# Attention and mixture-of-experts layer: gathers in bursts of eight, the last addition by banks, the last store on another queue

## The chip, the cores and the metric

The kernel runs on one core of one Trainium2 chip. Its time is the device time of one execution in microseconds (us); less is better. TensorE (PE in the profile) multiplies matrices into PSUM banks, VectorE (DVE) and ScalarE (ACT) work element by element, GpSimd (POOL) here makes the lists for indirect transfers, and SyncE (SP) issues the plain transfers. Each engine runs its own instructions in order; semaphores tie them together.

## The reference, cut to what matters

Inputs are x (2, 1024, 256), a context (2, 64, 256) and weights, all float32. First comes a cross-attention with 8 heads of 64, whose queries are x and whose keys and values are x and the context; its normalised output is added to x. The second part is the one that the change touches:

```python
x = x + _L0_xattn_ref(ctx_1024, _layernorm(x), mask, ...)
x = x + _L0_ffn_ref(_layernorm(x), ...)

# _L0_ffn_ref(x, ...)
shared_out = (silu(x @ shared_w1) * (x @ shared_w2)) @ shared_w3      # hidden width 1024
scores = sigmoid(x @ router_w)
_, top_idx = top_k(scores + expert_bias, 2)                           # 2 of 16 experts
gates = sum(one_hot(top_idx) * top_scores)
for each expert e:                                                    # hidden width 256
    routed_out += (silu(x @ w1[e]) * (x @ w2[e])) @ w3[e] * gates[:, e]
return shared_out + routed_out
```

The result for every token is its attention result, plus the shared branch, plus the gated results of its two experts.

## The kernel before, in words

The 2048 tokens are 16 tiles of 128 (`NT = 16`). Attention fills the span up to about 490 us and stays untouched. Behind it, the routed branch works on slots: the rows of the tokens are scattered in HBM so that the rows of one expert lie together (GpSimd, L714), 47 slots of 128 rows run through their expert's weights (about 635 to 777 us), and each slot's result is stored in the HBM tensor `slot_results`.

The shared branch has 32 steps n: four groups of 4 tiles (g = n // 8), and in each group 8 parts of the hidden width. A step is `hidden` (8 matmuls, L1062, about 3.4 us), then silu on ScalarE (L1317), then the product on VectorE (L1578), then `down` (8 matmuls, L1077, about 1.7 us), which adds to banks 4 and 5. `down(n)` is run behind `hidden(n + 1)`; behind the last `hidden`, n = 31, `down(30)` and `down(31)` run back to back. Steps 0 to 21 run before the slots. **Steps 22 to 31 run behind them (`BREAK = 22`), and they are the last stretch of the kernel: everything in the change lies there.**

Beside these ten steps the results come back. For each tile n GpSimd issues two gathers (`TOP = 2`, L724), 128 rows each, into one of three buffers (`NGAT = 3`), having waited until the tile three before was combined. VectorE's `combine(n)` (two instructions, L1761) waits for both gathers to land, multiplies by the gates and adds to `x2`. VectorE's order is written out: a product, then combines, up to tile 2j - 2 behind the product of step 22 + j. So tiles 13 and 14 are combined between the products of steps 30 and 31, and tile 15 behind the product of step 31. Last comes `add_shared(3)` (L1584), which waits for the last `down` and adds bank 4 (tiles 12 and 13), then bank 5 (tiles 14 and 15), with one signal behind both. SyncE waits for each tile's combine and stores the tile (L591); before tile 12 it waits for the last addition, so tiles 12 to 15 are stored at the very end.

The scatter loop (L714) waits behind every four tiles (`BURST = 4`), that is eight transfers, until all have landed. The gather loop has no such wait.

Of the kernel before, what the change touches and what calls it, by code (L numbers as in the profile page):

```python
# [29 lines left out]
B, S, D = 2, 1024, 256  # L30
# [3 lines left out]
P = 128  # L34
# [3 lines left out]
NT = B * TQ  # L38
# [8 lines left out]
SU = SH // P  # L47
# [4 lines left out]
NG = NT * P // GR  # L52
TOP = 2
NS = (TOP * NT * P + E * (P - 1)) // P
NGAT = 3
# [13 lines left out]
def wait(eng, sem, value):  # L69

    if isinstance(value, int) and value <= 0:
        return
    eng.wait_ge(sem, value)


def build(nc, x, ctx, mask, ln_x_w, ln_x_b, ln_l_w, ln_l_b, wq, wkv, q_scale, k_scale, wo,
          ln_o_w, ln_o_b, router_w, expert_bias, sw1, sw2, sw3, rw1, rw2, rw3, out, dbg=None):
    es = ExitStack()

    def sb(name, shape, dt=F32, stack=es):  # L80
        return stack.enter_context(nc.sbuf_tensor(name, shape, dt))

    def sem(name):
        return es.enter_context(nc.semaphore(name))
# [80 lines left out]
    x2 = sb("x2", [P, NT, D], stack=ffn)  # L165
# [5 lines left out]
    if nc.sbuf_bytes_remaining > att_end:  # L171
# [78 lines left out]
    hid_made, sil_ready, hid_ready, ysh_made, ysh_added = (sem("hid_made"), sem("sil_ready"), sem("hid_ready"),  # L250
                                                         sem("ysh_made"), sem("ysh_added"))
# [7 lines left out]
    gathered = [sem(f"gathered{i}") for i in range(NGAT)]  # L259
    combined, out_stored = sem("combined"), sem("out_stored")  # L260
# [148 lines left out]
    GB = NG - 1  # L409
# [8 lines left out]
    BURST = 4  # L418
# [40 lines left out]
    def _(sp):  # L459
# [125 lines left out]
        for n in range(NT):  # L585
            sp.wait_ge(combined, n + 1)
            if n == 4 * (GB - 1):
                sp.wait_ge(ysh_added, GB)
            if n == 4 * GB:
                sp.wait_ge(ysh_added, NG)  # L590
            sp.dma_start(out[n % B, (n // B) * P:(n // B + 1) * P, :], x2[:, n, :]).then_inc(out_stored, 16)  # L591
        sp.wait_ge(out_stored, 16 * NT)

# [2 lines left out]
    def _(pool):  # L596
        g = nc.gpsimd
# [68 lines left out]
        for m in range(NCH):  # L666
# [4 lines left out]
            n = TK * m  # L671
# [48 lines left out]
        for n in range(NT):  # L720

            wait(pool, combined, n - NGAT + 1)
            for k in range(TOP):
                g.indirect_dma_start(out=gat[n % NGAT][:, k, :], out_offset=None, in_=ys_dram,  # L724
                                     in_offset=bass.IndirectOffsetOnAxis(ap=posi[:, n, k:k + 1], axis=0)
                                     ).then_inc(gathered[n % NGAT], 16)
# [3 lines left out]
    def _(pe):  # L730
# [275 lines left out]
        def turn_xf(t):  # L1006
            pe.wait_ge(xf_ready, t + 1)
            if t == EARLY:
                pe.wait_ge(o_ready, NCH)
            if t > EARLY:  # L1010
                pe.wait_ge(xf_moved, t)
            for c in range(B):
                for k in range(DK):
                    last = nc.tensor.transpose(turn_bank(t)[:, (c * DK + k) * P:(c * DK + k + 1) * P],
                                               xf[:, 2 * t + c, k * P:(k + 1) * P], ident[:, :])
            last.then_inc(xf_turned, 1)
# [49 lines left out]
        def down(g, u, beside_pair=None):  # L1066
            pe.wait_ge(hid_ready, SU * g + u + 1)
            if g == 0 and u == 0:
                pe.wait_ge(o_ready, NCH)
            if g == 0 and u in (0, 2):  # L1070
                pe.wait_ge(w3s_loaded, 16 if u == 0 else 32)
            if u == 0:
                wait(pe, ysh_added, g)
            for j in range(4):
                if j == 2 and beside_pair is not None:
                    turn_xf(beside_pair)
                last = mm_(bank[4 + j // 2][:, (j % 2) * D:(j % 2 + 1) * D], hbuf[:, u % 4, j * P:(j + 1) * P],  # L1077
                           w3s[:, u, :], start=(u == 0 and j % 2 == 0), stop=(u == SU - 1), skip_group_check=True)
            if u == SU - 1:
                last.then_inc(ysh_made, 1)  # L1080

        def shared(n):

            g, u = divmod(n, SU)
            if u == 0:
                pe.wait_ge(xf_moved, 2 * g + 2)
            now, last = beside(n), beside(n - 2)
            if last == TQ - 1:
                route()
                turn_logits()  # L1090
            if now is not None and now <= EARLY:
                now = None
            if n == 1:
                pe.wait_ge(y_used, EARLY + 1)
            if n == COUNT_AT:
                count_tokens()
            hidden(g, u)
            if now is not None:
                project_o(now)
            for m in down_after(n):  # L1100
                down(*divmod(m, SU), beside(m) if m < n else None)
# [52 lines left out]
    def _(act):  # L1154
# [156 lines left out]
        def shared(n):  # L1311
            last = beside(n - 2)
            if last == TQ - 1:
                copy_logits()
                make_scores()
            act.wait_ge(hid_made, n + 1)
            a(hbuf[:, n % 4, :], hidden_bank(n, 0)[:, :], ACT.Silu).then_inc(sil_ready, 1)  # L1317
            if beside(n - 1) is not None:
                copy_xfT(beside(n - 1))
# [30 lines left out]
        for n in range(BREAK, SU * NG):  # L1350
            shared(n)


    @block.vector
    def _(dve):
# [224 lines left out]
        def add_shared(g):  # L1580
            dve.wait_ge(ysh_made, g + 1)
            for j in range(2):
                rows = x2[:, 4 * g + 2 * j:4 * g + 2 * j + 2, :]
                last = v.tensor_tensor(rows, bank[4 + j][:, :].rearrange("p (c d) -> p c d", c=2), rows, ALU.add)  # L1584
            last.then_inc(ysh_added, 1)
            v.drain()
# [30 lines left out]
        def shared_product():  # L1617

            nonlocal hid
            product(hid // SU, hid % SU)  # L1620
            if hid % SU == 0 and hid:
                add_shared(hid // SU - 1)
            hid += 1
# [150 lines left out]
        while done < NT:  # L1774
            combine(done)
            done += 1
        v.drain()
        add_shared(GB)

    es.close()  # L1780
# [26 lines left out]
```

## Time and profile before

| what | value |
|---|---|
| median of 3 runs | 833.82 us (833.03 to 834.02) |
| the profiled execution, its own time | 838.75 us |
| its span, first to last instruction | 837.0 us |
| TensorE busy | 806.2 us, 96% |
| VectorE, ScalarE, GpSimd busy | 58%, 41%, 39% |
| mean granted clock of TensorE | 0.996 of full |
| last stretch (ten shared steps, 16 tiles gathered and combined) | about 775.6 to 837.0 us |

The profiled execution is 4.93 us longer than the median of the ordinary runs. "Busy" leaves waits out; the view by chain follows the instruction that ended last back through what released it.

### The profile page before, as it was taken

Reading aid. Unit: us, or ns where it says so; the run is one execution under the profiler, and the core shown is the slowest. Engines: PE = TensorE matmul, PEld = TensorE weight load, DVE = VectorE, ACT = ScalarE, POOL = GpSimd, SP = SyncE. Lnnn points to the kernel's source line nnn. Section 1 sums busy time; section 2 is a strip of 40 time slices with the busy share of each in tenths; the row PEclk is TensorE's granted clock in tenths of the full one; section 3 lists DMA queues with packets and bytes.
Section 4 is the critical chain, followed back from the end, with each engine's and each line's share of the span. In section 5 each row is a group of like instructions: output and inputs, shape, how many; then the busy total and the mean of one; then the engine's idle time right before and its main releaser. Section 6 shows DMA issues by size and latency. Waiting matters only on the chain.

```text
span 837.0 us, 12969 instructions
## 1 busy us (share of the span) xinstructions
PE 806.2 (96%) x4354; PEld 492.8 (59%) x4355; DVE 485.8 (58%) x905; ACT 341.4 (41%) x652; POOL 327.0 (39%) x252
## 2 busy tenths in 40 slices
PE   8999988999999999999999999999999999999987
PEld 5444344545545554555454456666557999999544
DVE  4877777776676767777663376647212333433334
ACT  3545364465656555655655321131112333333110
POOL 3000034466665656465666743310661000000463
PEclk9999999999999999999999999999999999999998
DMA  3105600000000000000002002491521232322343
GB/s 114 36 29 182 227 1 1 14 14 14 14 9 7 14 14 14 15 15 14 14 17 74 13 25 63 145 325 64 183 89 64 94 94 89 93 90 79 89 131 95
DMA packets 54117, 55.99 MB, mean 67 GB/s; under 512 B 10666, under 2 KB 49204, under 8 KB 54068
## 3 DMA queue, kind: packets, MB, share of 16 engines
q1 hardware_dynamic: 50980, 46.96, 17.9%
q0 software_dynamic: 3072, 8.39, 3.1%
q8 instruction: 29, 0.48, 0.2%
q14 instruction: 20, 0.16, 0.1%
q10 hardware_dynamic: 16, 0.00, 0.0%
HBM read 36.60 MB, written 18.67 MB: 66 GB/s over the span
## 4 chain that ended last, share of the span: by engine, by line
PE 89%; ACT 4%; DVE 2%; POOL 1%; issue 1%; DVEq 1%; DMA 0%; ACTq 0%; POOLq 0%
PE bank L914 14%; PE bank L1062 13%; PE bank L888 11%; PE bank L762 11%; PE bank L1125 10%; PE bank L1077 7%; PE bank L842 5%; PE bank L1134 5%; PE bank L897 4%; ACT prob L1238 3%; PE bank L968 2%; PE bank L826 2%; PE bank L923 2%; PE bank L1115 1%; POOL acc L680 1%
## 5 line engine op out<-in xcount | busy, mean ns | idle before, releaser
L1238 ACT ACTIVATE prob<-bank,zero 128x512 f32<-128x512 f32 x256 | 158.7, 691 | 103.8 <-PE bank L897 103.2
L1446 DVE TENSOR_REDUCE mx<-bank 128x1 f32<-128x512 f32 x256 | 164.4, 686 | 54.2 <-PE bank L842 53.9
L680 POOL TENSOR_TENSOR acc<-acc,prob 128x1024 f32<-128x1024 f32 x64 | 152.1, 2377 | 26.4 <-ACT prob L1238 19.2
L914 PE MATMUL bank<-prob,vn 128*64 128x512 f32 x576 | 134.2, 601 | 0.6 <-DVE on L1511 0.6
L1062 PE MATMUL bank<-xfT,w12s 128*128 128x512 f32 x256 | 115.8, 596 | 1.8 <-DVE yn L1594 1.1
L724 POOL DMA_INDIRECT slot_result<-slot_results,posi x32 | 30.5, 954 | 165.6 <-DMA slot_results<-yo 147.0
L1125 PE MATMUL bank<-xsT,w_slot 128*128 128x128 f32 x752 | 91.9, 275 | 1.0 <-ACT xsT L1327 1.0
L1125 PEld LDWEIGHTS bank<-xsT,w_slot 128*128 128x128 f32 x752 | 89.2, 191 | 6.0 <-ACT xsT L1327 1.6
L686 POOL TENSOR_TENSOR acc<-acc,tail 128x1024 f32<-128x1024 f32 x16 | 38.1, 2381 | 109.9 <-DVE tail L1494 109.9
L1062 PEld LDWEIGHTS bank<-xfT,w12s 128*128 128x128 f32 x256 | 48.7, 192 | 51.8 <-issue 48.4
L914 PEld LDWEIGHTS bank<-prob,vn 128*64 128x64 f32 x576 | 37.2, 136 | 67.8 <-issue 46.0
L1317 ACT ACTIVATE hidden_units<-bank 128x512 f32<-128x512 f32 x32 | 19.0, 597 | 136.2 <-PE bank L1062 127.0
L888 PE MATMUL bank<-q_hi,k_hi 64*128 64x512 f32 x288 | 62.8, 431 | 8.0 <-ACT prob L1238 8.0
L842 PE MATMUL bank<-k_hi,q_hi 64*128 64x512 f32 x256 | 62.2, 481 | 5.7 <-DVE mx L1446 2.0
L1077 PE MATMUL bank<-w3s,hidden_units 128*128 128x256 f32 x256 | 62.0, 384 | 2.8 <-DVE hidden_units L1578 2.8
L1077 PEld LDWEIGHTS bank<-w3s,hidden_units 128*128 128x128 f32 x256 | 48.5, 192 | 19.8 <-issue 11.0
L1744 DVE TENSOR_TENSOR rgT<-hidden_units,bank 128x256 f32<-128x256 f32 x47 | 19.8, 421 | 68.3 <-ACT hidden_units L1332 68.3
L1578 DVE TENSOR_TENSOR hidden_units<-hidden_units,bank 128x512 f32<-128x512 f32 x32 | 21.9, 686 | 62.2 <-ACT hidden_units L1317 36.3
L897 PE MATMUL bank<-neg_max,ones_r 64*128 64x512 f32 x288 | 57.2, 392 | 0.0
L888 PE MATMUL bank<-q_hi,k_lo 64*128 64x512 f32 x288 | 57.1, 391 | 0.0
L888 PE MATMUL bank<-q_lo,k_hi 64*128 64x512 f32 x288 | 57.1, 390 | 0.0
L842 PEld LDWEIGHTS bank<-k_hi,q_hi 64*128 64x128 f32 x256 | 24.1, 183 | 53.7 <-DVE mx L1446 25.4
(171 smaller groups left out, 1105.1 us busy)
## 6 DMA issues: line engine op xcount, KB each, us to landing
w12r<-in_L_ffn_routed_w SPq DMA_DIRECT2D x32, 256.0 KB
slot_rows<-zrow SPq DMA_DIRECT2D x47, 128.0 KB, 1.9
xsl<-slot_rows SPq DMA_DIRECT2D x47, 128.0 KB, 2.1
slot_results<-yo SPq DMA_DIRECT2D x47, 128.0 KB, 1.7
w3r<-in_L_ffn_routed_w SPq DMA_DIRECT2D x16, 256.0 KB
rec<-row_sum_reciprocals SPq DMA_DIRECT2D x28, 128.0 KB, 2.8
xin<-in_x SPq DMA_DIRECT2D x16, 128.0 KB, 2.1
w12s<-in_L_ffn_shared_w SPq DMA_DIRECT2D x2, 1024.0 KB, 7.0
```

The costliest lines, as they stand in the source:

```text
L680: g.tensor_tensor(acc[:, m % 2, :, :], acc[:, m % 2, :, :], prob[:, (n + kt) % PROBS, :, :], ALU.add).then_inc(summed, 1)
L762: last = mm_(dst[:, :], xT_of(n, c)[:, k, :], wqkv[:, k, j * INNER:(j + 1) * INNER], start=(k == 0), stop=(k == DK - 1))
L842: mm_(two[h][:, :], q_hi[p][rows, t * P:(t + 1) * P], k_hi[p][rows, c * QC:(c + 1) * QC], start=True, stop=True).then_inc(ring_made, 1)
L888: mm_(two[h][:, :], lhs[rows, keys], rhs[rows, queries], start=(lhs is k_hi[p] and rhs is q_hi[p]), stop=False)
L897: mm_(two[h][:, :], ones_r[rows, :], neg_max[rows, queries], start=False, stop=True)\
L914: last = mm_(bank[O_BANK][rows, :], vn[:, kt, b, (2 * j + h) * DH:(2 * j + h + 1) * DH], prob[:, n % PROBS, h, :], start=(kt == 0), stop=( ...
L1062: last = mm_(hidden_bank(n, w)[:, :], w12s[:, k, w, u * P:(u + 1) * P], xfT[:, k, bass.ds(g * GR, GR)], start=(k == 0), stop=(k == DK - 1))
L1077: last = mm_(bank[4 + j // 2][:, (j % 2) * D:(j % 2 + 1) * D], hbuf[:, u % 4, j * P:(j + 1) * P], w3s[:, u, :], start=(u == 0 and j % 2 == ...
L1125: last = mm_(bank[2 + p][:, j * P:(j + 1) * P], w_slot[:, p, k, j * P:(j + 1) * P], xsT[:, p, k, :], start=(k == 0), stop=(k == DK - 1))
L1134: last = mm_(bank[6 + p][:, 0:D], rgT[:, p, k * P:(k + 1) * P], w3r[:, e, k, :], start=(k == 0), stop=(k == HID // P - 1))
L1238: a(prob[:, n % PROBS, h, :], bank[2 * (n % 2) + h][:, :], ACT.Exp, bias=bias).then_inc(probs_ready, 1)
L1446: v.tensor_reduce(mx[:, h, t, c:c + 1], ring_bank(u)[:, :], AX.X, ALU.max).then_inc(ring_used, 1)
```

## The change

Four edits, all in the last stretch. GpSimd, before the gathers of tiles 4, 8 and 12, waits until those of the tiles before have landed. TensorE signals bank 4 as soon as its last matmul there is issued, VectorE adds bank 4 on that signal and signals SyncE, then waits for the second signal and adds bank 5. SyncE stores tiles 12 and 13 behind the first of these additions and tile 14 behind the second. Tile 15 is stored by ScalarE, behind its last silu.

```diff
@@ block.sync
             if n == 4 * GB:
                 sp.wait_ge(ysh_added, NG)
+            if n == 4 * GB + 2:
+                sp.wait_ge(ysh_added, NG + 1)
+            if n == NT - 1:
+                break
             sp.dma_start(out[n % B, (n // B) * P:(n // B + 1) * P, :], x2[:, n, :]).then_inc(out_stored, 16)
@@ block.gpsimd
             wait(pool, combined, n - NGAT + 1)
+            if n and n % BURST == 0:
+                for last in range(n - NGAT, n):
+                    pool.wait_ge(gathered[last % NGAT], 16 * TOP * (last // NGAT + 1))
             for k in range(TOP):
                 g.indirect_dma_start(out=gat[n % NGAT][:, k, :], ...)
@@ block.tensor, down(g, u)
+                if g == GB and u == SU - 1 and j == 1:
+                    last.then_inc(ysh_made, 1)
             if u == SU - 1:
                 last.then_inc(ysh_made, 1)
@@ block.scalar, behind the last step
+        act.wait_ge(combined, NT)
+        act.wait_ge(ysh_added, NG + 1)
+        act.dma_start(out[(NT - 1) % B, (NT - 1) // B * P:, :], x2[:, NT - 1, :]).then_inc(out_stored, 16)
@@ block.vector, add_shared(g)
             for j in range(2):
+                if g == GB and j == 1:
+                    last.then_inc(ysh_added, 1)
+                    dve.wait_ge(ysh_made, g + 2)
                 rows = x2[:, 4 * g + 2 * j:4 * g + 2 * j + 2, :]
                 last = v.tensor_tensor(rows, bank[4 + j][:, :].rearrange("p (c d) -> p c d", c=2), rows, ALU.add)
```

`GB` is 3, `NG` is 4, `SU` is 8, `B` is 2.

## Rows read from the trace of the kernel before

**Rows 1.** Page, part 1: busy us, share of span, instructions.
```profile
PE 806.2 (96%) x4354; PEld 492.8 (59%) x4355; DVE 485.8 (58%) x905; ACT 341.4 (41%) x652; POOL 327.0 (39%) x252
```
**Rows 2.** Waits of PE, whole span: us in total, times, longest us.
```profile
PE bank L888 <- ACT prob L1238: 8.0, 18, 0.6
PE bank L1077 <- DVE hidden_units L1578: 2.8, 1, 2.8
```
**Rows 3.** Chain that ended last, in order: start us, us, work.
```profile
782.61 1.73 PE bank L1077 x8
...
808.41 1.73 PE bank L1077 x8
810.14 4.79 PE bank L1062 x8
816.32 2.91 PE bank L1077 x8
819.23 4.21 PE bank L1062 x8
823.44 1.73 PE bank L1077 x8
...
828.60 3.47 PE bank L1077 x16
```
**Rows 4.** Timeline of ACT, last stretch: start us, us, work, idle before.
```profile
803.29 0.60 ACT L1317 ACTIVATE hidden_units<-bank 128x512 f32<-128x512 f32 x1 [4.56 <-issue]
814.95 1.09 ACT L1317 ACTIVATE hidden_units<-bank 128x512 f32<-128x512 f32 x2 [11.06 <-PE bank L1062]
```
**Rows 5.** By windows: us, busy of PE, PEld, DVE, ACT, POOL, clock, DMA share, GB/s.
```profile
817.00:821.00 4.00, 4.00 (x10) 2.42 (x9) 2.61 (x6) 0.00 (x0) 2.84 (x3) 0.57 0.43 112
```
**Rows 6.** Timeline of POOL, the gathers.
```profile
786.92 0.95 POOL L724 DMA_INDIRECT slot_result<-slot_results,posi  x1 [0.30 <-issue]
792.23 0.94 POOL L724 DMA_INDIRECT slot_result<-slot_results,posi  x1 [4.36 <-DVE x L1761]
...
800.98 0.95 POOL L724 DMA_INDIRECT slot_result<-slot_results,posi  x1 [0.30 <-issue]
...
803.48 0.95 POOL L724 DMA_INDIRECT slot_result<-slot_results,posi  x1 [0.30 <-issue]
...
811.12 0.94 POOL L724 DMA_INDIRECT slot_result<-slot_results,posi  x1 [0.30 <-issue]
...
823.75 0.94 POOL L724 DMA_INDIRECT slot_result<-slot_results,posi  x1 [0.30 <-issue]
```
**Rows 7.** Timeline of DVE, last stretch.
```profile
806.19 1.04 DVE L1761 SCALAR_TENSOR_TENSOR x<-slot_result,gate,x 128x256 f32<-128x256 f32 x2 [0.63 <-DMA slot_result<-slot_results,posi]
...
826.55 1.04 DVE L1761 SCALAR_TENSOR_TENSOR x<-slot_result,gate,x 128x256 f32<-128x256 f32 x2 [0.80 <-DMA slot_result<-slot_results,posi]
829.26 0.69 DVE L1578 TENSOR_TENSOR hidden_units<-hidden_units,bank 128x512 f32<-128x512 f32 x1 [1.67 <-ACT hidden_units L1317]
829.87 1.03 DVE L1761 SCALAR_TENSOR_TENSOR x<-slot_result,gate,x 128x256 f32<-128x256 f32 x2
832.09 1.29 DVE L1584 TENSOR_TENSOR x<-bank,x 128x512 f32<-128x512 f32 x2 [1.19 <-PE bank L1077]
```
**Rows 8.** Line 714, the scatters in bursts: idle before it until.
```profile
  DMA slot_rows<-xf,posi: 7.3, 3
```
**Rows 9.** SP's stores: line 591 as a whole, and the last two in time.
```profile
L591 SPq DMA_DIRECT2D out<-x x16: 332/332/458, 784.9 to 834.8; - x16
...
834.30 0.95 SPq L591 DMA_DIRECT2D out<-x  x2
```
**Rows 10.** Timeline of ACT at the start: one store issue of its queue.
```profile
1.66 0.28 ACTq L1159 DMA_DIRECT2D sq<-in_L_xattn_ln_x_w  x1
```
**Rows 11.** Page, part 6: transfer, KB each, median us to landing.
```profile
rec<-row_sum_reciprocals SPq DMA_DIRECT2D x28, 128.0 KB, 2.8
```

## The prediction, made before the changed kernel ran

> **What bounds the kernel now.** I read the shares first: TensorE is busy 806.2 of 837.0 us [rows 1]. Then TensorE's own waits, to see what is not work: 8.0 us in 18 short waits of the attention, which the change doesn't touch, and one single wait of 2.8 us, of `down` for VectorE's product [rows 2]. Then the chain in order of time, to see where that one lies and what ends the kernel. In the last stretch the chain is TensorE alone. From 782.61 to 808.41 five steps take 25.80 us, 5.16 each. Then comes one irregular place. `down(28)` would begin at 808.41 + 5.16 = 813.57 and begins at 816.32, 2.75 late; it lasts 2.91 instead of 1.73, and the `hidden` behind it 4.21 instead of 3.43 (5.16 - 1.73) [rows 3]. The granted clock of that place is 0.57, partly the lower of the two levels (1.2 GHz) [rows 5], behind 2.75 us without a matmul. So this place costs 2.75 + 1.18 + 0.78 = 4.71 us.
>
> Its cause isn't arithmetic. ScalarE's silu follows the end of `hidden` at once in the other steps; for step 28 it should begin near 803.29 + 5.16 = 808.45, but it begins at 814.95, together with that of step 29, and the releaser is TensorE's `hidden` [rows 4], which by the chain was long done. TensorE's signal reached ScalarE 6.5 us late. GpSimd had issued gathers without a pause from 792.23 to 812.06 [rows 6]. That is coincidence or cause; the trace can't tell.
>
> **Which of the two times holds this place.** The profiled execution took 838.75 us, the ordinary ones 833.82. The difference is 4.93; the irregular place is 4.71. TensorE is at work nearly everywhere else, at full clock, so an ordinary execution has hardly another place to be 4.9 us shorter. I conclude that the ordinary runs most likely don't have the late signal. The sum below is therefore made on the profiled execution with its late part drawn forward by 4.71: TensorE's last matmul ends at 828.60 + 3.47 - 4.71 = 827.36, the span at 837.0 - 4.71 = 832.29, the time at 838.75 - 4.71 = 834.04, which is 0.22 from the median.
>
> **Last addition and stores.** Before: both additions take 1.29 us behind the last matmul [rows 7], then SyncE issues four stores, the third at 834.30 and the last at 834.8, and the span ends 2.2 later [rows 9]. After: bank 4 is complete four matmuls earlier, 4 x 0.217 = 0.87 us, so its addition (about 0.65) fits in front of the last matmul's end if VectorE is free, and stores 12 and 13 issue meanwhile. Behind the last matmul stands one addition: 832.09 + 0.69, a hand-over of 0.07, and both last stores issue at 832.85, one on each queue. The last issue moves from 834.8 to 832.85: **a gain of 1.95 us, if VectorE is free.** ScalarE's store waits behind nothing: its last silu is over 3 us earlier. The trace shows its queue in use at 0.28 us an issue [rows 10], against 0.33 to 0.46 on SyncE [rows 9], so I cost the move at nothing; bounds are 0 and +0.5 (a SyncE slot with its gap), and cover is the equal issue of tile 14 beside it.
>
> On the second queue the page "DMA: Bandwidth & Descriptors" of the Trainium skill, section "Issuing engines are not separate DMA queues", speaks against a large gain: the same 16 engines move the data, and only the issue time is saved. By that rule the edit is worth one issue slot, 0.50 (834.8 - 834.30), which is what the sum above gives it. No row of before shows two queues storing at once.
>
> **The waits between bursts.** Gathers start every 1.25 us (0.95 of work and 0.30 between) [rows 6]. The landing counts from the end of a tile's second issue to the start of a combine that waited for it. Tile 8: issue over at 804.43, combine at 806.19, 1.76. Tile 14: 824.69 and 826.55, 1.86 [rows 6, 7]. The bursts of the scatters idle 7.3 us in 3 waits, 2.43 each [rows 8], which with a hand-over of 0.26 is a landing of 2.17. I take 1.85, since gathers are the same transfers in the same place; bounds are 1.5 and 2.17.
> - Before tile 4: the eighth issue ends at 787.87 and would be landed near 789.7; GpSimd waits for a combine until 792.23 anyway. Cost nothing, and 2.5 us of cover.
> - Before tile 8: the issue of tile 7 is over at 801.93. Landing 1.85 and hand-over 0.26 let tile 8 start at 804.04 instead of 802.23: 1.81 late. Its four tiles are issued by 804.04 + 9.70 = 813.74.
> - Before tile 12: again 1.85 + 0.26; tile 12 starts at 815.85. Without the irregular place and without waits it would be 812.2. Tile 14 is issued by 823.05, landed at 824.90; tile 15 by 825.55, landed at 827.40.
>
> Queued behind the waiting instruction on GpSimd are only the later gathers; who waits for these is VectorE, and **in its order the product of step 31 stands behind the combine of tile 14.** ScalarE's silu lets that product begin at 829.26 - 4.71 = 824.55. The combine of tile 14 begins at 824.90 and takes 1.04 (a product can start 0.1 before its end): product at 825.86, 1.31 late. `down(31)` has room: it starts 1.73 behind `down(30)`, at 830.33, and the product ends at 829.95 [rows 3, 7]; 0.38, less a hand-over, 0.3. So TensorE waits 1.0 us and ends at 828.4. I cost no clock loss: 1.0 us is far less than the 2.75 behind which rows 5 show one. Earlier products are late by at most 1.6 (step 30, behind tile 12), where `down` leaves 3.5; this is hidden.
>
> Then the end: tile 15 is landed at 827.40 and combined at 828.45; only now VectorE adds bank 4 (to 829.15) and bank 5 (to 829.8). SyncE issues store 12 at 829.2, 13 at 829.6, 14 at 830.05; ScalarE's tile 15 goes at 829.85. End 830.05 + 2.2 = 832.25, against 832.29. **The waits take back what the edits of the tail bring: -0.05, that is -0.1 with rounding, 833.82 - 0.1 = 833.7.**
> With landing 1.5: tile 8 starts at 803.7, tile 14 is landed at 823.85 and tile 15 at 826.35; TensorE isn't held, the additions end near 828.6, the end is 831.1: -1.2, 832.6. With landing 2.17: tile 14 landed at 825.85, product 2.3 late, TensorE ends at 829.4, end 833.2: +0.9, 834.7. These are the bounds of the likeliest case.
>
> **The rivals.**
> 1. *The late signal is in the ordinary runs too, and the pauses prevent it.* For: it came behind some 16 gathers in a row, and no burst of eight shows one. Against: the agreement of 4.93 with 4.71. Then 833.82 - 4.7 - 0.1 = 829.0.
> 2. *The waits cost nothing on the path* (landings of 1.2 or less, or gathers that run ahead): 833.82 - 1.95 = 831.9. No landing in the trace is so short.
> 3. *Slower: the gathers become the bound.* If a gather beside the stores of the output takes as long as the 2.8 us of the `rec` transfers [rows 11], the two waits and the last landing add 0.95 each to the case above: tile 14 is landed at 827.75, TensorE waits near 3.9, more than the 2.75 behind which the clock fell, and `down(31)` takes 2.91 as in rows 3. Additions end at 833.2, the end is near 835.45: +3.2, 837.0. It decides from a landing of about 2.3, where the clock loss sets in, and 835.5 is passed.
> 4. *The change doesn't do what it says*: the wait before tile 4 is already idle time, so only two of the three waits exist; that is in the sum.
>
> **How the numbers follow.** Likeliest case 0.70, 833.7, own range 832.6 to 834.7. Rival 1: 0.13 at 829.0. Rival 2: 0.08 at 831.9. Rival 3: 0.09 at 835.5 to 837. The range reaches to rival 2 and to the near side of rival 3: 831.7 to 835.2; left out are rival 1 and most of rival 3, 0.2. About 0.2% (1.67 us) is what a measurement of this kernel can tell from no change. Faster than 832.15: rival 1 and the greater part of rival 2, 0.19. Slower than 835.49: 0.08. Same: 0.73.
>
> **What would show it.** GpSimd idle about 2.1 us before the 17th and 25th gather and nothing new before the 9th; the product of step 31 released by the combine, not by silu; TensorE idle about 1 us before the last 8 matmuls; the last two additions back to back behind the combine of tile 15, not around the last matmul; two stores at the end within 0.3 us. The profiled span should fall by more than the median, to about 832, if the late signal is gone there. Wrong would be made of me: a median near 829 (rival 1), or TensorE without a wait at step 31 (rival 2).

## The result, and the profile after

In the comparison of the result the changed kernel took 835.33 us (median of 10, 834.43 to 836.67) and the kernel before 833.44 (10 runs, 832.4 to 835.13). The ratio is 1.0024, interval 1.0014 to 1.0034: 1.9 us slower, where 0.1 us faster was forecast. The profiled execution took 835.03 us with a span of 833.3.

The waits of TensorE in the last stretch of the changed kernel (us in total, times, longest), to be held against [rows 2]:

```profile
PE bank L1084 <- DVE hidden_units L1591: 2.5, 1, 2.5
```

There is one wait again, of nearly the same length, but at another place. GpSimd's timeline of the changed kernel, around its two new pauses:

```profile
799.64 0.95 POOL L731 DMA_INDIRECT slot_result<-slot_results,posi  x1 [0.30 <-issue]
803.17 1.11 POOL L731 DMA_INDIRECT slot_result<-slot_results,posi  x1 [2.58 <-DMA slot_result<-slot_results,posi]
...
812.18 0.94 POOL L731 DMA_INDIRECT slot_result<-slot_results,posi  x1 [0.30 <-issue]
815.69 1.10 POOL L731 DMA_INDIRECT slot_result<-slot_results,posi  x1 [2.57 <-DMA slot_result<-slot_results,posi]
...
822.10 0.95 POOL L731 DMA_INDIRECT slot_result<-slot_results,posi  x1 [0.30 <-issue]
```

Then VectorE and ScalarE, from the combine of tile 11 to the end:

```profile
814.93 1.04 DVE L1777 SCALAR_TENSOR_TENSOR x<-slot_result,gate,x 128x256 f32<-128x256 f32 x2 [0.85 <-DMA slot_result<-slot_results,posi]
...
824.85 1.04 DVE L1777 SCALAR_TENSOR_TENSOR x<-slot_result,gate,x 128x256 f32<-128x256 f32 x2 [1.45 <-DMA slot_result<-slot_results,posi]
825.81 0.68 DVE L1591 TENSOR_TENSOR hidden_units<-hidden_units,bank 128x512 f32<-128x512 f32 x1
827.40 1.04 DVE L1777 SCALAR_TENSOR_TENSOR x<-slot_result,gate,x 128x256 f32<-128x256 f32 x2 [0.90 <-DMA slot_result<-slot_results,posi]
828.66 0.69 DVE L1600 TENSOR_TENSOR x<-bank,x 128x512 f32<-128x512 f32 x1 [0.22 <-PE bank L1084]
830.05 0.69 DVE L1600 TENSOR_TENSOR x<-bank,x 128x512 f32<-128x512 f32 x1 [0.70 <-PE bank L1084]
...
822.39 0.60 ACT L1326 ACTIVATE hidden_units<-bank 128x512 f32<-128x512 f32 x1 [4.56 <-PE bank L1069]
830.83 0.39 ACTq L1364 DMA_DIRECT2D out<-x  x1
```

TensorE's last matmuls, and the clock by windows (us, busy of PE, clock, DMA share, GB/s):

```profile
822.19 1.89 PE L1084 MATMUL bank<-w3s,hidden_units 128*128 128x256 f32 x8
826.55 3.46 PE L1084 MATMUL bank<-w3s,hidden_units 128*128 128x256 f32 x8 [2.46 <-DVE hidden_units L1591]
...
826.15:829.56 3.41, 3.01 (x7) 0.50 0.12 38
```

The reader should follow one line. The silu of step 31 begins at 822.39, on time, 5.16 behind the one before. Its product could begin 0.63 later, at 823.02, and begins at 825.81, right behind the combine of tile 14. TensorE, which could go on at about 824.1, waits 2.46 us. Behind the wait its clock is at the lower level (0.50), and the last eight matmuls take 3.46 us; behind a like wait at full clock they take 1.99 (e4 shows the lines). So the mechanism that the prediction summed is there, at the predicted place; its sizes are not.

### The profile page after: what moved, and what is told of

It is laid out like the page before. It is cut to its first block, busy times and chain, and to the rows that moved or that the text cites. A ratio compares the mean times of both kernels' runs of the same rounds, so it can differ in the third digit from the quotient of the medians.

```text
span 833.3 us, 12978 instructions
## 1 busy us (share of the span) xinstructions
PE 805.2 (97%) x4354; PEld 493.6 (59%) x4355; DVE 485.6 (58%) x905; ACT 341.4 (41%) x652; POOL 327.7 (39%) x252
## 4 chain that ended last, share of the span: by engine, by line
PE 87%; ACT 3%; DVE 3%; POOL 2%; DMA 2%; issue 1%; DVEq 0%; ACTq 0%; POOLq 0%
PE bank L921 15%; PE bank L895 12%; PE bank L769 11%; PE bank L1134 10%; PE bank L1069 10%; PE bank L1084 5%; PE bank L849 5%; PE bank L1143 5%; PE bank L904 4%; PE bank L975 3%; ACT prob L1247 3%; POOL slot_result L731 2%; PE bank L833 2%; PE bank L930 2%; DMA slot_result<-slot_results,posi 1%
## 5 line engine op out<-in xcount | busy, mean ns | idle before, releaser
L679 POOL TENSOR_TENSOR acc<-prob 128x1024 f32<-128x1024 f32 x16 | 37.8, 2364 | 45.0 <-ACT prob L1247 45.0
```

## The experiments

**The kernel before comes in two kinds of session.** A session is a set of runs on one chip, the kernel before among them. The medians of that kernel were:

| session | kernel before, us | span of its executions | what ran beside it |
|---|---|---|---|
| 1 (the result) | 833.44 | not on record | the changed kernel: 835.33 |
| 2 | 837.54 | 833.9 to 837.4 | parts of the change |
| 3 | 837.87 | 834.2 to 837.6 | the changed kernel: 835.63 |
| 4 | 837.47 | 833.6 to 837.1 | another order of combines |
| 5 | 833.53 | 830.7 to 832.4 | the changed kernel: 835.31 |
| 6 | 837.50 | 833.9 to 837.0 | parts, and the kernel before again |
| 7 | 833.15 | 830.8 to 832.7 | the tail edits alone |

The spans of the two kinds don't overlap. The changed kernel takes the same in both. Sessions 5 and 7 were on one chip, 2, 3, 4 and 6 on four others. The traces below show what lengthens the kernel in the second kind: the late signal of [rows 4]. No trace of the kernel before in the faster kind exists; e16 stands in for it.

The two kinds differ in their traces even where no signal is late. The changed kernel in session 3 (e5), then in session 5 (e11), in the list of transfers:

```profile
slot_result<-slot_results,posi POOLq DMA_INDIRECT x32
slot_result<-slot_results,posi POOLq DMA_INDIRECT x32, 2.7
```

The first has no time to landing, since part of the landings' semaphore updates isn't in the trace. All fourteen traces of sessions 2, 3, 4 and 6 are like that, and so is the first trace of the kernel before; they hold 8247 to 8403 semaphore updates. The three others (the first trace after, e11 and e16) hold 9068 to 9071. So the profile that the prediction was made on is of the kind with late signals, and session 1 is of the other.

**e1: the tail edits alone.** From the changed kernel:
```diff
-            if n and n % BURST == 0:
-                for last in range(n - NGAT, n):
-                    pool.wait_ge(gathered[last % NGAT], 16 * TOP * (last // NGAT + 1))
```


> The changed kernel without GpSimd's waits: only the bank-by-bank addition and the last store on ScalarE's queue. Theory A (the waits cost, the tail edits gain): TensorE has no wait in the last stretch, the last issue comes 1.95 us earlier than in the kernel before, so 0.9977 of it, near 831.5 us. Theory B (the tail edits themselves cost, by the second queue or the split addition): 1.000 or more. Theory C (late signals of TensorE behind an unbroken row of gathers are also in ordinary runs): some executions near 4.7 us longer, with a mean clock near 0.996, in this kernel and in the one before.

Session 2: 836.64 us, 0.9994 of the kernel before (0.9984 to 1.0004). Its ScalarE timeline:

```profile
802.13 0.60 ACT L1323 ACTIVATE hidden_units<-bank 128x512 f32<-128x512 f32 x1 [4.56 <-issue]
813.82 1.08 ACT L1323 ACTIVATE hidden_units<-bank 128x512 f32<-128x512 f32 x2 [11.09 <-PE bank L1066]
```

The silu of step 28 is 6.5 us late (802.13 + 5.16 = 807.29), as in the first trace, and every one of the 12 executions has a span of 833.7 or more. So the late signal isn't an accident of one execution. Theory C held, and for all executions, where it expected some; the 0.9977 of theory A had to wait for e16.

**e2: the waits alone.** GpSimd's part of the change, in the kernel before.

> The kernel before with GpSimd's waits alone. Theory A: TensorE waits 2.5 us before the last down and runs it at the lower clock (1.7 us more), as in the changed kernel, and additions and four stores follow in full: the changed kernel's time plus 1.9, 1.0047 of the kernel before, near 837.3. Theory B: the waits cost nothing, 1.000.

Session 2: 836.38 us, 0.9987 (0.9978 to 0.9995). Neither theory gave that, since both left out that the kernel before has the late signal here: the waits remove it and cost nearly as much. TensorE waits 2.3 us at step 31, the clock falls behind it, and no silu is late:

```profile
826.34 3.19 PE L1080 MATMUL bank<-w3s,hidden_units 128*128 128x256 f32 x8 [2.26 <-DVE hidden_units L1581]
```

**e3: the last product ahead of tiles 13 and 14.**
```diff
-            while done < min(NT, 2 * (n - BREAK) - 1):
+            while done < min(NT, 2 * (n - BREAK) - 1, 13 if n < SU * NG - 1 else NT):
```


> The changed kernel, but VectorE computes the product of step 31 ahead of the combines of tiles 13 and 14. Theory A (that product is what TensorE waits for, and behind it the landing of tile 15 is the next bound): no wait and no lower clock at TensorE, but the combine of tile 15 still starts near the same time, so only 0.8 us of the 4.2 come back: about 834.6, 1.0014 of the kernel before. Rival (the product's place is all of the loss): all 4.2 come back, 831.3, 0.9975.

Session 2: 834.98 us, 0.9969 (0.9959 to 0.9978) of a kernel before that takes 837.54. VectorE's timeline:

```profile
823.78 0.69 DVE L1591 TENSOR_TENSOR hidden_units<-hidden_units,bank 128x512 f32<-128x512 f32 x1 [1.45 <-ACT hidden_units L1326]
...
828.12 1.04 DVE L1777 SCALAR_TENSOR_TENSOR x<-slot_result,gate,x 128x256 f32<-128x256 f32 x2 [1.43 <-DMA slot_result<-slot_results,posi]
829.25 1.29 DVE L1600 TENSOR_TENSOR x<-bank,x 128x512 f32<-128x512 f32 x2
```

The product follows the silu, TensorE has no wait in the last stretch. But the combine of tile 15 still waits for its landing, and both additions follow it. The absolute time is near the 834.6 of theory A, 0.3 to 0.7 below the changed kernel in sessions 5 and 3 (in session 2 that one wasn't run). So taking away TensorE's wait alone gives back little: the late last landing, on a path beside it, holds the end nearly as far.

**e4: TensorE kept busy.**
```diff
         def down(g, u, beside_pair=None):
+            if SU * g + u == SU * NG - 1:
+                for _ in range(11):
+                    nc.tensor.transpose(bank[7][:, 0:P], ident[:, :], ident[:, :])
```


> The changed kernel with 11 transposes of the identity (0.21 us each, into a bank that is free) ahead of the last down, where TensorE otherwise waits; their result isn't used. Theory A (the last eight matmuls are slow because TensorE stood still before them): they take 1.73 us instead of 3.46, TensorE ends near the combine of tile 15, and 0.8 us come back: 1.0014 of the kernel before. Rival (they are slow for another reason, such as VectorE's use of memory or the end of the kernel): 3.46 us, as the changed kernel or 0.1 slower, 1.0024.

Session 2: 834.53 us (5 runs), 0.9964 (0.9951 to 0.9976). TensorE:

```profile
825.46 1.36 PE L1076 MATMUL bank<-ident 128*128 128x128 f32 x11
828.99 2.60 PE L1087 MATMUL bank<-w3s,hidden_units 128*128 128x256 f32 x8 [2.17 <-DVE hidden_units L1594]
```

The transposes took 1.36 us together, not 2.3, so TensorE still stood for 2.17 and the clock still fell, though later; the eight matmuls took 2.60. The profiled execution was the slowest of the five (836.6), so it isn't a typical one. The median is in line with theory A, but the run doesn't separate it cleanly. Three other traces show that the fall is not fixed to the wait: two of the changed kernel (e5, e11) and e7.

```profile
828.18 1.99 PE L1084 MATMUL bank<-w3s,hidden_units 128*128 128x256 f32 x8 [2.48 <-DVE hidden_units L1591]
826.64 1.99 PE L1084 MATMUL bank<-w3s,hidden_units 128*128 128x256 f32 x8 [2.55 <-DVE hidden_units L1591]
829.15 1.99 PE L1084 MATMUL bank<-w3s,hidden_units 128*128 128x256 f32 x8 [3.28 <-DVE hidden_units L1591]
```

The granted clock of these eight is 1.00 in e5 and e11. **The clock loss of the first trace after (3.46 instead of 1.99) is therefore one that comes in some executions.**

**e5 and e11: the changed kernel again, in two more sessions.**

> The changed kernel itself, beside the kernel before once more. Theory L (TensorE's signal is held back while a row of well over eight gathers is in flight; it happens in all executions of the kernel before in one session and in nearly none in another, and the changed kernel never has it): where the kernel before takes 837.5 the changed one stays near 835.3, so 0.9974 of it; where the kernel before takes 833.4, 1.0024. Rival (the hold-up is chance, or comes with any kernel alike): 1.0024 in every session.

> The changed kernel once more, in another session. What is open is when the kernel before has the late signals: in the comparison of the result it took 833.4 us, in three sessions since 837.5 to 837.9. Theory S (it is a state of the session, such as the place of the tensors or the chip): the kernel before is either near 833.4 or near 837.6, not between, and the changed one is near 835.4 both times, ratio 1.0024 or 0.9975. Rival (chance in every execution): the executions of the kernel before are mixed.

Session 3: 835.63 us, 0.9976 of the kernel before (0.9965 to 0.9988). Session 5: 835.31 us, 1.0020 (1.0011 to 1.0029). The sign of the change depends on the session, as theory L and theory S said; within a session the kernel before isn't mixed.

**e6 and e7: one wait only.**
```diff
-            if n and n % BURST == 0:
+            if n == 3 * BURST:        # e6;  n == 2 * BURST in e7
```


> The changed kernel with only the last of the three waits, before tile 12. Tiles 4 to 11 are again sixteen gathers in a row. Theory L: where the kernel before has the late signal this one has it too, at step 28, and equals the kernel with the tail edits alone, 0.9994 to 0.9977 of the kernel before; TensorE has no wait at step 31. Where the signals are in time, a single wait is covered (product of step 31 late by 0.3, which is the room that down has), 0.9977. Rival (any one wait is enough against the late signal): 4.7 less than before on top of the 1.9, 0.992.

> The changed kernel with only the wait before tile 8: rows of eight gathers and then sixteen (tiles 8 to 15), these up to about 825. Theory L: the sixteen begin 12 us later than in the kernel before, so the hold-up can strike only the last signals, step 30 or 31, and ends when the last gathers have landed near 826; a loss of 0 to 3.5 us. If none strikes: 0.9977 of the kernel before where that has its signals in time, 0.992 where it hasn't. Rival (the number of gathers isn't what matters): late at step 28 as before.

Session 3, where the kernel before has late signals. e6: 836.08 us, 0.9979 (0.9967 to 0.9992); e7: 836.49 us, 0.9985 (0.9975 to 0.9994). ScalarE in e6, then in e7:

```profile
802.32 0.60 ACT L1326 ACTIVATE hidden_units<-bank 128x512 f32<-128x512 f32 x1 [4.56 <-issue]
814.04 1.09 ACT L1326 ACTIVATE hidden_units<-bank 128x512 f32<-128x512 f32 x2 [11.12 <-PE bank L1069]
```
```profile
813.87 0.60 ACT L1326 ACTIVATE hidden_units<-bank 128x512 f32<-128x512 f32 x1 [4.56 <-PE bank L1069]
820.63 0.60 ACT L1326 ACTIVATE hidden_units<-bank 128x512 f32<-128x512 f32 x1 [6.17 <-remote]
827.78 0.60 ACT L1326 ACTIVATE hidden_units<-bank 128x512 f32<-128x512 f32 x1 [6.55 <-remote]
```

With the row of sixteen left as tiles 4 to 11, the late signal stays at step 28. With the row moved to tiles 8 to 15, it moves with it: step 28 is on time, step 30 is 1.6 late, step 31 by 3.6. So it belongs to a long unbroken row of gathers, not to a place of the program. The rival that any one wait is enough falls. In e7 a landing is late too: the second gather of tile 14 is issued by 822.41 and its combine starts 3.2 us later, where 1.80 is usual. But its transfers took 1.7 us instead of 0.8 and ended about 1.0 us late (824.84), so this needn't be the same hold-up.

```profile
825.62 1.04 DVE L1777 SCALAR_TENSOR_TENSOR x<-slot_result,gate,x 128x256 f32<-128x256 f32 x2 [2.71 <-DMA slot_result<-slot_results,posi]
```

How long the row must be, the traces bound: in the first trace step 27 was in time with 9 gathers of the row begun, step 28 late with 13; in e7 step 29 was in time with 7, step 30 late with 12.

**e8: waits that leave two gathers in flight.**
```diff
-                for last in range(n - NGAT, n):
+                for last in range(n - NGAT, n - 1):
```


> The changed kernel, its waits asking for the tile before the last only, so that two gathers remain in flight and GpSimd hardly pauses. Theory W (what the change pays for is the full landing and GpSimd's start after it, 2.6 us each time): no idle time over 0.6 at tiles 8 and 12, product of step 31 in time. Theory L then says that the row is unbroken, so the late signal is back where the kernel before has it: 0.9994 of it, or 0.9977 where that has none. Rival (the waits help by holding GpSimd back at all): signals in time, 0.992.

Session 3: 836.63 us, 0.9991 (0.9978 to 1.0003). In the trace GpSimd issues tiles 4 to 11 every 1.25 us again, and step 28 is late (ScalarE at 813.62 in place of 807.21). It is the real pause that keeps the signals in time. That the pauses are also what costs, e16 shows, and e9 that they do so by making the last landing late.

**e9 and e14: combines earlier, so that the pauses cost nothing.**
```diff
-            while done < min(NT, 2 * (n - BREAK) - 1):
+            while done < {SU * NG - 3: 13, SU * NG - 2: 14}.get(n, min(NT, 2 * (n - BREAK))):
```


> The changed kernel with another order on VectorE: behind the product of step 22 + j it combines up to tile 2j - 1 instead of 2j - 2 (so tile 1 is combined early, and the gathers of tile 4 can start near 790.4 instead of 792.3), but behind the products of steps 29 and 30 only up to tiles 12 and 13, so that no gather is waited for ahead of the last product. Theory A + L (the waits keep the signals in time, and their price is only that the last gathers land late): no wait of TensorE, last landing about 1.9 us earlier than in the changed kernel, last stretch 56.0 us from TensorE's first step 22 to the end: about 3.2 us less than the changed kernel, 832.1. Against the kernel before 0.9985 where that has its signals in time, 0.9935 where it hasn't. Rival (VectorE becomes late elsewhere, since it waits for tiles earlier): 835 or more.

> The changed kernel with the earlier combines. If the kernel before is near 833.4: the span is as on the other chip, since no signal is late in either, near 832.9, 0.9994 of it: the order gives back what the waits cost, and the rest is the tail's gain. If it is near 837.6: 0.9944 as before.

Session 4: 833.06 us, 0.9944 (0.9930 to 0.9958). Session 6: 833.14 us, 0.9953 (0.9940 to 0.9965). GpSimd, then VectorE in e9:

```profile
788.98 0.94 POOL L731 DMA_INDIRECT slot_result<-slot_results,posi  x1 [2.55 <-DMA slot_result<-slot_results,posi]
825.49 1.04 DVE L1777 SCALAR_TENSOR_TENSOR x<-slot_result,gate,x 128x256 f32<-128x256 f32 x2 [0.82 <-DMA slot_result<-slot_results,posi]
```

GpSimd resumes at tile 4 behind a landing (idle 2.55) instead of behind a combine (4.37), no silu is late, TensorE has no wait, and the last tile's combine begins at 825.49, 1.9 earlier than in the first trace after. All three pauses are kept. The time is 2.2 to 2.6 us below the changed kernel's 835.3 to 835.6 of other sessions, where 3.2 was expected. This is the best of the kernels where signals are late; where they are in time it wasn't run, and the 0.9994 forecast for it stays open.

**e10: the same order without the waits.**

> The same order without GpSimd's waits. Now nothing breaks the row of gathers from the first tile on. Theory L (a row of more than about ten gathers holds TensorE's signals back until it ends): the first late signal comes earlier than at step 28, at step 25 or 26, near 793 to 798, and the last stretch is as long as in the kernel before or longer. Rival (the hold-up belongs to a fixed place of the program, such as the fetch of ScalarE's or TensorE's code near step 28): late at step 28 again. If no signal is late: 831, as no wait costs anything.

Session 4: 836.63 us, 0.9989 (0.9977 to 1.0002). ScalarE:

```profile
797.06 0.60 ACT L1323 ACTIVATE hidden_units<-bank 128x512 f32<-128x512 f32 x1 [4.56 <-PE bank L1066]
803.38 0.60 ACT L1323 ACTIVATE hidden_units<-bank 128x512 f32<-128x512 f32 x1 [5.73 <-PE bank L1066]
813.97 1.09 ACT L1323 ACTIVATE hidden_units<-bank 128x512 f32<-128x512 f32 x2 [9.99 <-PE bank L1066]
```

The first late signal is one step earlier (step 27 by 1.2 us, step 28 by 6.6), not at step 25 or 26 as expected. GpSimd had a pause of 1.75 us before tile 5; what that does to the count wasn't tested. The direction is theory L's, its "more than about ten" in this form isn't shown.

**e12, e13, e15: tail edits alone, waits alone and the kernel before once more.** The kernels of e1 and e2, and the unchanged one.

> The tail edits alone, once more. If the kernel before is near 833.4 here (signals in time): the last issue comes 1.9 us earlier, less 0.35 for two stores landing at once, 0.9981 of it, near 831.8. If it is near 837.6, as the first time: 0.998 to 0.9994. Rival (the split addition or the second queue costs): 1.000 or more.

> The waits alone, once more. If the kernel before is near 833.4: the waits cost TensorE 2.5 us before the last eight matmuls and, when the clock falls behind it, up to 1.7 more, so 2.5 to 4.2: 1.0030 to 1.0050 of it, near 836.7. If it is near 837.6, as the first time 0.9987.

> The kernel before itself, for its trace. If it is near 833.4: all ten silus of the last stretch follow their hidden at once, 5.16 us apart, GpSimd gathers from 792 to 822 without a pause, TensorE never waits, and the last stretch (from TensorE's step 22 to the end) is 56.7 us instead of 61.4. If it is near 837.6: the silu of step 28 is 6.5 late as in the first trace. Ratio 1.000 either way.

Session 6, late signals again: 836.11 us, 0.9988 (0.9979 to 0.9997); 836.95 us, 0.9989 (0.9980 to 0.9999); 837.91 us, 1.0007 (0.9996 to 1.0018). The first two repeat session 2. The third says what two copies of one kernel differ by here, and its trace has the silu of step 28 late by 6.4 us. But the clock isn't lost behind it there, and the silu of step 31 is only 2.9 us late, where e1 has 4.7: the late place costs 3 to 5 us by execution.

**e16: the tail edits alone, signals in time.**

> The tail edits alone, a third time, since both sessions so far had late signals. If the kernel before is near 833.4 here: 0.9981 of it, near 831.8 (last issue 1.9 us earlier, less 0.35 for the two last landings), so that the waits cost the difference to the changed kernel's 1.002, 0.4% or 3.5 us. If it is near 837.6: 0.9988 to 0.9994, as twice before. Rival (the tail edits bring nothing or cost): 1.000 or more where it is near 833.4, and the waits then cost only 2 us.

Session 7, kernel before 833.15: 831.50 us, 0.9978 (0.9969 to 0.9987). ScalarE and, below, SyncE and ScalarE's queue:

```profile
802.12 0.60 ACT L1323 ACTIVATE hidden_units<-bank 128x512 f32<-128x512 f32 x1 [4.56 <-PE bank L1066]
807.28 0.60 ACT L1323 ACTIVATE hidden_units<-bank 128x512 f32<-128x512 f32 x1 [4.56 <-PE bank L1066]
812.44 0.60 ACT L1323 ACTIVATE hidden_units<-bank 128x512 f32<-128x512 f32 x1 [4.56 <-PE bank L1066]
...
826.12 1.31 SPq L595 DMA_DIRECT2D out<-x  x3
826.99 0.40 ACTq L1361 DMA_DIRECT2D out<-x  x1
```

The program is that of e1 and e12, its gathers run from 791.06 to 821.39 without a pause, twenty-four in a row, and all signals are in time. So a long row alone isn't enough for the late signal: the session decides. The tail edits are worth 0.22%, 1.8 us. The changed kernel stands at 1.0020 and 1.0024 in such sessions, so **the waits cost 1.0020 / 0.9978 = 1.0042, 3.5 us** (3.8 by the two medians on this chip, 835.31 and 831.50).

## Why the prediction was wrong

**That ordinary runs have their signals in time** was right for the session of the result, and worked out from a trace that had them late: the place costs 4.71 there, and the two kinds of session differ by 4.2 (837.5 to 837.9 against 833.2 to 833.5). That the 4.93 agreed so closely was partly luck: the executions of the late kind spread over 4 us, and this one had lost the clock as well. Rival 1 is what happens in the other sessions. Its mechanism (the pauses prevent the late signal) was right, its time of 829.0 wasn't: it took the 4.7 off 833.82, a time without late signals, and carried the same too small price of the waits. The changed kernel takes 835.6 there.

**The last addition and the stores** were right: 1.95 forecast, 1.8 measured alone (e16). The last issue came 1.9 earlier, 0.8 behind the last matmul instead of 2.7; the two stores issued at once then took 2.6 us to the end (829.6 - 826.99) instead of the 2.2 behind [rows 9]. This fits the Trainium skill ("DMA: Bandwidth & Descriptors", "Issuing engines are not separate DMA queues"): a second queue saves issue time only.

**The landing** was sized right: tile 11 was issued by 813.12 and combined from 814.93, 1.81 us, and tile 14 took 1.80, where 1.85 was taken.

**The hand-over to GpSimd is the term that failed.** The prediction took 0.26 us between a landing and GpSimd's next gather. In the trace after, tile 11 is landed at 814.93 at the latest, by VectorE's start, and GpSimd begins at 815.69, 0.76 later (0.79 behind the landing as recorded, 814.91; the same before tile 8); its first gather then takes 1.10 instead of 0.95. The pause is 2.57 and 2.58 instead of 2.11. Per pause that is 0.46 + 0.15 = 0.6 us, for two 1.2, and one slower gather before them (1.14 us) adds 0.2. The product of step 31 was 2.79 late where 1.31 was forecast.

The prediction also misread the row that it took for a bound. The 2.43 of [rows 8] is the mean of three unequal pauses, in the trace before:

```profile
598.30 0.95 POOL L714 DMA_INDIRECT slot_rows<-xf,posi  x1 [3.92 <-DMA slot_rows<-xf,posi]
609.80 0.96 POOL L714 DMA_INDIRECT slot_rows<-xf,posi  x1 [1.69 <-DMA slot_rows<-xf,posi]
621.31 0.96 POOL L714 DMA_INDIRECT slot_rows<-xf,posi  x1 [1.70 <-DMA slot_rows<-xf,posi]
```

The trace after gives the scatters 2.4 us from issue to landing, 0.96 of it the issue:

```profile
slot_rows<-xf,posi POOLq DMA_INDIRECT x32, 2.4
```

So a scatter lands about 1.4 us after its issue, and a pause of 1.69 leaves a hand-over of about 0.3: there the 0.26 was right. No row of before could show the 0.76, since no gather waited for a landing in it. The trace after shows one difference between the two. A scatter carries its only wait itself. Before tile 12 GpSimd has four waits; those for the landings are in separate instructions, the last of which ends at 814.97, 0.72 before the gather starts, and the gather carries the wait for the combine. Tile 8 has the same 0.72. Whether the order of the waits is the cause wasn't tested.

**The room behind it** was right (0.3), so TensorE waits 2.46 instead of 1.0.

**The clock was the second miss.** It was costed at nothing, since 1.0 us is far from the 2.75 of rows 5. With 2.46 it is lost in some executions: 3.46 - 1.99 = 1.47 us in the first trace after, nothing in those of sessions 3 and 5. Where it isn't lost, the end has the form that was forecast, the two additions back to back behind the combine of tile 15; where it is, TensorE ends last. VectorE in e11, where it isn't:

```profile
827.32 1.04 DVE L1777 SCALAR_TENSOR_TENSOR x<-slot_result,gate,x 128x256 f32<-128x256 f32 x2 [0.73 <-DMA slot_result<-slot_results,posi]
828.46 1.29 DVE L1600 TENSOR_TENSOR x<-bank,x 128x512 f32<-128x512 f32 x2
```

**The sum.** Forecast: waits +1.9, tail -1.95. Measured: waits +3.5, tail -1.8, together +1.7 and +1.9. The last landing accounts for most of the error. The silus of the first steps begin 1.53 us earlier in the trace after than in the one before (777.68 and 779.21 for step 22), so the forecast 827.40 for the combine of tile 15 means 825.9 there. It began at 827.40 (827.32 in e11), 1.5 late, and the two stores at once add 0.4. The slower rival described this course (gathers that land late, a wait of TensorE, then the clock), but asked for landings of 2.3 us or more; it was the pause, not the landing, that was longer. Its chance of 0.09 was too small: the sum's two terms nearly cancelled, so that an error of 1.5 us in either decided the sign.

**What stays open** is what in a chip or session makes the signals late, and by which path gathers hold them back. No run here could turn that on or off. One rival stands untested: in the late kind part of the semaphore updates is missing from the traces, so the delay may have to do with the recording of updates and not with the signals as such. That ScalarE waited for code rather than for the signal is excluded: the update itself is recorded at 814.93 in the first trace, 0.02 before the silu.

## What to carry to other kernels

A hand-over taken from one kind of wait (0.27 to 0.3 us here) needn't hold for another (0.76): where no row has the same wait, put the hand-over into the range as well as the landing. Look at each pause before using their mean. When such a pause delays a transfer, go on to the instruction that stands behind its consumer in order, and count its room; then move that instruction ahead, or start the transfers earlier, as e9 did: it kept the pauses and won 2.2 to 2.6 us over the changed kernel, though on other chips and only where signals are late. And when a profiled execution is longer than the ordinary ones by the size of one irregular place, look on more than one chip before trusting either.

## What the runs showed of the hardware

- **TensorE's signals can be held back while GpSimd's gathers run in a long row.** In four sessions on four chips every execution of the kernel before has a span of that kind (108 executions, 833.6 us or more); in two sessions on another chip none has (30 executions, 832.7 at most). TensorE itself goes on until it needs an answer to the signal. In seven traces (first, e1, e6, e8, e10, e12, e15) the signals of steps 28 and 29 came within 0.2 us of each other, the first of them 6.4 to 6.6 us late, 1.3 to 1.4 us behind the end of the last gather's transfers (in the first trace 814.93 and 813.50). In part this is a circle: the row ends there because GpSimd waits for a combine that stands behind the late silu. It isn't always so: step 27 of e10 (1.2 late) and step 30 of e7 (1.6 late) got their signals while gathers went on.
- GpSimd starts 0.76 to 0.79 us after the landing that it waited for with an instruction of its own, and its first gather takes 1.10 us (tiles 8 and 12 of the trace after); behind a combine's signal, which the gather itself waits for, it went on 0.27 us after the combine's end (tile 4), and behind a scatter's landing, which the next scatter waits for itself, after about 0.3.
- The clock may or may not fall behind a stand of 2.5 us of TensorE: last eight matmuls 3.46 us in one trace of the changed kernel, 1.99 in two. Nor does the length of the stand settle it: behind 2.17 (e4) and 2.26 (e2) it fell, behind 3.28 (e7) the eight took 1.99.
